# A macaron block on one Trainium2 core: the recurrent cell worked in column halves, with its operands taken straight from PSUM

## The reference

```python
def ffn(x):                                    # x: (2, 4096, 512)
    S  = slot_init * slot_scale                # 64 slots x 512, the same for both batches
    h  = gelu(cat(x, mean(S)) @ w1.T + b1)
    alpha = top-8 softmax of (h @ w2.T + b2) / (|tau| + 0.1)       # (2, 4096, 64)
    gi = einsum('bts,btd->bsd', alpha, x) / (alpha.sum(1) + 1e-8)  # 128 rows x 512
    gx, gh = gi @ gru_wih.T + gru_bih, S @ gru_whh.T + gru_bhh
    r, z = sigmoid(xr + hr), sigmoid(xz + hz)
    n  = tanh(xn + r * hn)
    S_new = (1 - z) * n + z * S
    return alpha @ (S_new @ wv.T + bv) @ wo.T + bo
x = x + 0.5 * ffn(layernorm(x)); x = x + attention(layernorm(x)); x = x + 0.5 * ffn(layernorm(x))
```

## Time and profile before

| | us |
|---|---|
| median of 3 runs | 3148.35 |
| lowest, highest | 3143.83, 3149.79 |
| the profiled execution's own time | 3147.79 |
| its span, first to last instruction | 3146.0 |
| PE busy, DVE busy | 2772.3, 1968.4 |
| ACT busy, POOL busy | 1034.5, 1333.4 |

### The profile page before, as it was taken

One profiled execution on the slowest core, in us unless ns is written; L12 is line 12 of the kernel. 1 busy time (PEld: TensorE's weight loads), 2 busy tenths in 40 slices (PEclk: granted clock), 3 DMA queues, 4 the chain that ended last, 5 costly groups with the idle time before them and its releaser, 6 DMA issues.

```text
span 3146.0 us, 119389 instructions
## 1 busy us (share of the span) xinstructions
PE 2772.3 (88%) x51036; PEld 1964.7 (62%) x51036; DVE 1968.4 (63%) x5236; ACT 1034.5 (33%) x1891; POOL 1333.4 (42%) x1768
## 2 busy tenths in 40 slices
PE   7999788888898999989989988999888999888867
PEld 5786456666666666666666666666666666666553
DVE  6776456566666666666666665666666666666625
ACT  5775223233333332323233322333333332323220
POOL 2221344444444444444445544544454444444410
PEclk9999899999999999999999999999999999999978
DMA  6341122222111222212222222222111222211177
GB/s 220 96 154 48 39 53 58 53 58 57 44 43 53 58 58 57 58 52 56 50 58 58 56 53 58 58 54 55 39 51 54 58 58 58 61 50 48 40 247 282
DMA packets 365979, 224.93 MB, mean 71 GB/s; under 512 B 277584, under 2 KB 294032, under 8 KB 365456
## 3 DMA queue, kind: packets, MB, share of 16 engines
q1 hardware_dynamic: 356240, 200.51, 23.1%
q10 hardware_dynamic: 9216, 16.78, 1.4%
HBM read 125.49 MB, written 74.97 MB: 64 GB/s over the span
## 4 chain that ended last, share of the span: by engine, by line
PE 51%; DVE 31%; issue 11%; POOL 2%; DMA 2%; ACT 1%; SPq 1%; DVEq 0%; POOLq 0%; ACTq 0%
DVE blk L3164 12%; PE psum L887 10%; DVE blk L3162 9%; PE psum L1067 4%; PE psum L983 4%; PE psum L1086 4%; PE psum L1008 4%; PE psum L1043 4%; PE psum L1053 4%; PE psum L963 2%; PE psum L1021 2%; PE psum L1107 2%; PE psum L942 2%; POOL sm L2490 1%; PE psum L791 1%
## 5 line engine op out<-in xcount | busy, mean ns | idle before, releaser
L887 PE MATMUL psum<-w_all,xnT 128*128 128x512 f32 (+2 forms) x2048 | 747.7, 501 | 16.5 <-DVE xc L3061 12.3
L2490 POOL TENSOR_TENSOR sm<-sm,half 128x1 f32<-128x1 f32 (+1 forms) x384 | 537.4, 1399 | 146.1 <-ACT sm L2065 130.1
L887 PEld LDWEIGHTS psum<-w_all,xnT 128*128 128x128 f32 x2048 | 364.4, 191 | 185.9 <-issue 140.5
L3164 DVE TENSOR_TENSOR blk<-blk 128x30 f32<-128x30 f32 (+14 forms) x960 | 452.4, 471 | 33.0
L3162 DVE TENSOR_TENSOR blk<-blk 128x30 f32<-128x30 f32 (+14 forms) x960 | 362.4, 378 | 69.7 <-issue 42.8
L942 PEld LDWEIGHTS psum<-xnT,w_all 128*128 128x128 f32 x2048 | 268.3, 200 | 80.5 <-issue 76.1
L942 PE MATMUL psum<-xnT,w_all 128*128 128x128 f32 x2048 | 292.8, 289 | 7.8 <-issue 7.8
L1067 PE MATMUL psum<-qg,st 32*32 32x64 f32 x8192 | 189.0, 227 | 92.2 <-DVE st L3180 51.7
L1086 PE MATMUL psum<-w_out,gate 128*128 128x512 f32 x512 | 264.4, 636 | 1.2 <-issue 1.0
L1067 PEld LDWEIGHTS psum<-qg,st 32*32 32x32 f32 x8192 | 143.8, 111 | 174.4 <-issue 167.5
L3180 DVE STREAM_TRANSPOSE st<-psum 128x128 f32<-128x128 f32 x256 | 81.0, 316 | 230.3 <-PE psum L1067 227.3
(11 more groups left out here) (276 smaller groups left out, 4694.8 us busy)
## 6 DMA issues: line engine op xcount, KB each, us to landing
blk<-n_scratch SPq DMA_DIRECT2D x64, 512.0 KB, 4.4
xin<-in_L_attn_x_dram SPq DMA_DIRECT2D x96, 256.0 KB, 4.2
xh<-xc SPq DMA_DIRECT2D x64, 256.0 KB, 2.3
n_scratch<-nn SPq DMA_DIRECT2D x64, 256.0 KB, 3.5
e_scratch<-blk SPq DMA_DIRECT2D x32, 512.0 KB, 2.6
E<-e_scratch SPq DMA_DIRECT2D x64, 256.0 KB, 3.9
x_scratch<-xh SPq DMA_DIRECT2D x62, 256.0 KB, 2.6
rxn<-in_L_attn_x_dram SPq DMA_DIRECT2D x32, 256.0 KB, 2.8
```

The lines of the kernel that those rows point to most:

```text
L887: last = mm(dst, xnT[b][:, k * P:(k + 1) * P], w_all[:, k * WK + at:k * WK + at + n], start=(k == 0), stop=(k == KC - 1))
L2490: return g.tensor_tensor(dst, a, half[:, 0:n], ALU.pow)
L3164: ins = tt(Y[:, 0:rows, s_ + 1:CH], Y[:, 0:rows, s_ + 1:CH], o, ALU.add)
```

## The change

The cell works in halves of 256 columns (`HC`) where a step waits for a step. The scaling reads the sums directly from PSUM, in two instructions; the transposes go two blocks at a time into two different banks (`turned`), and ACT copies each half. The z product is made as two products of 256 columns into two banks (`z_at`), and its sums, sigmoids and the last two DVE operations are done by halves. The bias of n is added to r times h_n ahead of the n product's end instead of behind it. `value(k)` are the four blocks of the last product. The last step's slot sums no longer go through ACT and POOL: DVE adds them out of PSUM. The memsets of `slotacc`, `st` and `sums` move from behind the first cell into it. ACT gets two 1x1 activations (`ask`), which place the table loads for Gelu and Exp in the last step of the attention pass.

```diff
+        turned = [Bk[0], C[1]]
+        z_at = [A[1][:, 0:HC], ST[0][:, 0:HC]]
...
                 e.wait_ge(mid_dve, o_dve + 1)
                 e.wait_ge(aT, NT * (m + 1))
-                for k in range(KC):
-                    last = tr(Bk[0][:, k * P:(k + 1) * P], ht[:, k * P:(k + 1) * P], ident[:, :])
-                last.then_inc(mid_pe, 1)
-                e.wait_ge(mid_act, o_act + 1)
+                turn(0)
+                e.wait_ge(mid_dve, o_dve + 2)
+                turn(1)
...
+                gate_product(A[0][:, :], 0, 0, D)
+                gate_product(C[0][:, :], 2, 0, D)
+                gate_product(z_at[0], 1, 0, HC)
+                gate_product(z_at[1], 1, HC, HC)
                 e.wait_ge(mid_dve, o_dve + 7)
+                turn(0)
+                e.wait_ge(mid_act, o_act + 7)
+                value(0)
+                e.wait_ge(mid_dve, o_dve + 8)
+                turn(1)
+                value(1)
+                e.wait_ge(mid_act, o_act + 8)
+                value(2)
+                value(3).then_inc(mid_pe, 1)
...
-            sp.wait_ge(mid_pe, 6 + 4)
+            sp.wait_ge(mid_pe, 9 + 6)
...
+                if n == NT and b == 0:
+                    act(ask[0:1, 0:1], eps[0:1, 0:1], ACT.Gelu).then_inc(asked, 1)
...
-            def slot_sums(m, rows, total):
-                ve.wait_ge(last_sums, m + 1)
-                own(v.tensor_copy(slotacc[:, D:D + 1], total))
-                own(v.tensor_copy(slotacc[:, 0:D], rows))
...
+                for c in (lo, hi):
+                    ts(ht[:, c], rows[:, c], s(0, "rden"), None, ALU.mult).then_inc(mid_dve, 1)
+                if m == 0:
+                    own(v.memset(slotacc[:, 0:D], 0.0))
+                    for b in range(B):
+                        own(v.memset(st[b][:, :], 0.0))
+                    own(v.memset(sums[:, :], 0.0))
...
-            ve.wait_ge(S["sla"], NT)
+            ve.wait_ge(S["sla"], NT - 1)
+            ve.wait_ge(S["slot_ps"], both(NT, 1))
+            own(tt(slotacc[:, 0:D], slotacc[:, 0:D], slot_at[:, :], ALU.add))
```

More of the change, by code:

```diff
@@ L81, in build @@
         eps = sb("eps", 1)
+        ask = sb("ask", 1)
         h_bias = sb("h_bias", 2)
@@ L338, in build, with turn, gate_product, value @@
         NMID = 4
+        HC = D // 2
+        turned = [Bk[0], C[1]]
+        z_at = [A[1][:, 0:HC], ST[0][:, 0:HC]]
         def mid(e, m):
-            o_pe, o_act, o_dve = 6 * m, 5 * m, 7 * m
+            o_pe, o_act, o_dve = 9 * m, 8 * m, 9 * m
             if e is nc.tensor:
                 mm, tr = nc.tensor.matmul, nc.tensor.transpose
+                def turn(h):
+                    for k in range(2):
+                        last = tr(turned[h][:, k * P:(k + 1) * P], ht[:, (2 * h + k) * P:(2 * h + k + 1) * P], ident[:, :])
+                    last.then_inc(mid_pe, 1)
+                def gate_product(dst, j, c, n):
+                    for k in range(KC):
+                        if j == 0 and k % 2 == 0:
+                            e.wait_ge(mid_act, o_act + 1 + k // 2)
+                        last = mm(dst, giT[:, k * P:(k + 1) * P], wihT_at(k, j)[:, c:c + n], start=(k == 0), stop=(k == KC - 1))
+                    last.then_inc(mid_pe, 1)
+                def value(k):
+                    return mm(Bk[1][:, :], hTT[:, k * P:(k + 1) * P], voT_at(k), start=(k == 0), stop=(k == KC - 1))
@@ L358, in mid @@
[L358 to L366, removed]
@@ L373, in mid @@
+                e.wait_ge(mid_dve, o_dve + 3)
                 act(gr[:, :], gr[:, :], ACT.Sigmoid).then_inc(mid_act, 1)
-                e.wait_ge(mid_dve, o_dve + 3)
+                e.wait_ge(mid_dve, o_dve + 4)
                 act(gn[:, :], gn[:, :], ACT.Tanh).then_inc(mid_act, 1)
[L376 to L379, removed]
+                for h in range(2):
+                    e.wait_ge(mid_dve, o_dve + 5 + h)
+                    act(gz[:, h * HC:(h + 1) * HC], gz[:, h * HC:(h + 1) * HC], ACT.Sigmoid).then_inc(mid_act, 1)
@@ L381, in _ @@
+                for h in range(2):
+                    e.wait_ge(mid_pe, o_pe + 7 + h)
+                    act(hTT[:, h * HC:(h + 1) * HC], turned[h][:, 0:HC], ACT.Copy).then_inc(mid_act, 1)
         @block.sync
@@ L2116, in last_exp @@
             def last_exp(n, b):
+                if n == NT and b == 0:
+                    act(ask[0:1, 0:1], eps[0:1, 0:1], ACT.Exp).then_inc(asked, 1)
                 sc.wait_ge(S["top"], both(n + NT, b))
@@ L2609, in slot_add @@
             def slot_add(n):
+                if n == NT:
+                    return
                 pl.wait_ge(S["slc"], n)
@@ L3704, in _ @@
             for b in range(B):
-                own(v.memset(st[b][:, :], 0.0))
                 own(v.memset(D33[b][:, :, 0:1], 0.0))
-            own(v.memset(sums[:, :], 0.0))
             first_dve()
```

56 lines of the change are left out of this document (27 added, 29 removed).

## The result

| | runs | median us | lowest, highest |
|---|---|---|---|
| before | 4 | 3149.07 | 3143.83, 3152.06 |
| after | 4 | 3111.75 | 3108.68, 3117.82 |

The ratio is 0.9886, 95% interval 0.9865 to 0.9907. The forecast was 3139.3, with a range from 3134.0 to 3146.0. Of all executions reported here, four between 5174 and 12049 us were disturbed and are left out. The profiled execution of the changed kernel took 3109.64 us and has a span of 3107.8, against 3146.0 before, 38.2 less.

The account below looks back on a forecast made before the run. One engine works at a time through each cell, so cuts there leave the total: 1.49 + 1.84 + 0.64 + 1.28 + 1.84 = 7.1 us, plus 2.0 for the clock, 9.1 us. Forecast 3139.3, range 3134 to 3146.

Parts of the forecast that it names:

- First cell, entry: First cell, DVE's first copy to the first product pass: scaling from PSUM and half transposes and copy gain 1.49 us.
- First cell, tail: First cell, end of the products to the last product: half operations gain 2.06 us, less 0.22 for two transposes: 1.84.
- Behind the first cell: Between first cell and the attention pass's first sum: moving DVE's 1.87 us of memsets away gains 0.64 us.
- Second cell, entry: Wait into the second cell and its steps before the products: DVE starts 0.25 us earlier, 1.28 us gained in all.
- the store that is late next: Ahead of the second cell: SP's store of the tile before, 4.9 us to land, holds ACT's `aT_out` copy; 0.28 more without it.
- Second cell, tail: Second cell, end of the products to the last product: gain 2.30 us, less 0.46 for two slow transposes: 1.84.
- The clock: PE's products in both cells: shorter gaps give back 0 to about 7 us lost to half clock; 2 us taken.
- The rival that the clock stays up in both cells: Both cells: shortened gaps no longer cost a half-clock stretch, 7.1 + 6 or 7 us, about 3135; chance 0.12.
- The rest: ACT's early table loads for Gelu and Exp: 0 us for both, bounds -0.3 and 0.
- The attention pass: The 32 steps between the cells: no gain counted; a shift of PE's instruction stream should average out.
- a rival for the worse: Attention pass: shifted PE instruction fetch makes the steps slower, at 0.5 us a step 3155; chance 0.08 that it eats the gain.
- a little luck: Attention pass: a favourable shift of PE's stream, as much luck as the other way, left within the forecast's range.

Follow-up runs that it names:

- The tiles' place: Kernel before plus only the unused one-column tile `ask` behind `eps`, moving every tile behind it by 32 bytes: 12.9 ± 2.8 us faster, ratio 0.996.
- The 16 instructions: Kernel before plus 16 PE semaphore signals of no effect in the first cell's gap behind the z product: 5.7 ± 2.1 us faster, ratio 0.998.
- The trace with a gap of 3.28 us: Changed kernel with the first cell's z product left whole instead of in halves: 24.7 ± 4.1 us faster than the kernel before, ratio 0.9922.

## Why the prediction was wrong

**What holds the time together.** The three comparisons of the changed kernel (36.0, 27.6 and 30.4), weighted by their errors, give 32.7 ± 1.9 us. One pair of traces gave 14.9 to the cells and what lies behind them, but parts of the second cell differ from execution to execution, so I take the means over all traces: the first cell gives 7.2 and the second 5.7, together 12.9. The tiles' place gives 12.9 ± 2.8 in the kernel before, 0.8 of it in the last loop. The 16 instructions give 5.7 ± 2.1 there. The sum is 31.5 ± 3.5. The first two parts are clear of noise. The third rests on a difference of 2.7 errors and on other shifts of the stream that gave other times. In the changed kernel the tiles' place is worth 32.7 - 14.4 = 18.3 ± 3.0, which leaves less for the stream; the two splits agree within their errors and no better.

**First cell, entry: right.** 1.91 and 1.34 us became 0.94 and 0.91, gain 1.40; forecast 1.49.

**First cell, tail: right.** 4.35 us became 2.28, less 0.22 for the transposes inside the last product: 1.85; forecast 1.84.

**Behind the first cell: right.** From the last product's end to the first sum, 2.64 us became 1.99 (319.17 to 321.16): 0.65; forecast 0.64. The moved memsets are hidden.

**Second cell, entry: the place was right, the size was not.** The steps in the cell gained 0.38 and 0.54, forecast 0.34 and 0.69. I named the store that is late next, and it was. But I gave it the 4.9 us of the earlier trace rows, and it took 6.94; why is not shown. From PE's last slot product DVE's start comes after 5.93 us, where it was 4.02 (3065.85 in the trace of before, to 3069.87): in this pair 1.9 later and not 0.25 earlier. Over all traces it is neither: from that product to DVE's reciprocal it is 4.4 to 7.3 us in the 12 with the cell of before and 4.4 to 6.7 in the 6 with the changed cell and the shared tile, 5.6 in the mean of each.

**Second cell, tail: right.** 4.81 us became 2.28, less 0.22: 2.31; forecast 1.84, because I reckoned with slow transposes and they ran at full clock. In 4 of the 12 traces with the cell of before they ran at full clock there too, so the mean gain is 2.2.

**The clock: mechanism right, term mis-sized.** The prediction said "I take 2 us, nearer to nothing". In the pair of traces it is 6.7: products 1.57 and 1.20, last products 1.69 and 2.27. In the means over all traces it is 5.9: 1.6 and 0.6, 1.7 and 2.0. The rival that the clock stays up in both cells gave 6 to 7, and it is what happened, but for the second cell's first products, which it had against it. My reason for only 2 us was that "where PE's clock changes relative to the work differs from execution to execution". In the first cell that is wrong. In all 12 traces with the cell of before, its products took 12.0 to 12.3 us and the last product, from first start to last end, 5.40. In the 7 with the cell of after and z in halves these are 10.59 and 3.92 each time. In the second cell it is right for the products: 12.0 to 13.4 us before and 11.7 to 12.9 after. The last product there took 5.4 to 6.0 before and 3.92 after, each time. The trace with a gap of 3.28 us shows the other side of the step. The Trainium skill (TensorE: Matmul & The Clock Gate, the HAM clock gate) says that the clock follows PE's recent activity; the traces agree, and I should have let its rival weigh more.

**The rest: right.** The load for Gelu is hidden before and after, and neither `ask` shows in the chain but for 0.2 us ahead of the last exponentials.

**The attention pass: the step that failed.** The cells gave 12.9 us by the means, and that alone would have put the time at 3135.5, inside the range. The other 19.8 ± 1.9 come from the pass, but for 0.8 in the last loop. The prediction put the pass at no change and had only a rival for the worse on it. It said of PE's stream that "the pattern already falls at other places in each step, so a shift should average out". The runs speak against it. A step has 3131 instructions, 59 more than a multiple of 256, so the edges do wander through the step. The share of stalls at the edges stays the same (103 of 210 and 107 of 198). Yet 16 more brought 6 us, 64 more cost 7 and 6 at two places of the program (the second not clear of noise once the late start is taken off), and 16 beyond the changed kernel's cost 10 to 12. Perhaps a wandering pattern repeats in 32 steps too seldom to even out; no run shows that. And since I thought of it only as a loss, its gain was left to "a little luck".

The larger part, 12.9 ± 2.8 us for the tile's 32 bytes, the prediction did not consider at all. It treated `ask` as two activations and not as a tile that moves 64 others. The diff shows its line, and the load's packets of 128 bytes were there to be looked at.

**Open.** Which accesses lose when the tiles lie 32 bytes beside a multiple of 64. E's load is one, 0.7 us each, but it brought only 3.4 ± 2.5 us. The store from `nn` and the last loop are two more; the three don't add up to 12.9 in the time. Nor is it known which edge of a block costs what in a step; I know the sums, not the places.

## What to carry to other kernels

A new tile, however small, is an edit to every tile behind it. Read the addresses of before and after modulo 64, try an unused tile first when a kernel moves 128-byte packets, and put small tiles last or together.

In a kernel whose PE runs tens of thousands of small instructions, a change in their number ahead of a long loop can move its time by several microseconds either way. Each shift here was only just clear of its noise, so this is a reading and not a law. A gain or loss of 0.2% in such a kernel is no verdict on the edit until the same edit has been timed with the stream shifted.

Where one engine works at a time, measure the gap ahead of a dense stretch, not only its work: here 2.3 us instead of 3.3 kept the clock and was worth more than the operations saved.

## What the runs showed of the hardware that was not expected

The 256 KB load of E in packets of 128 bytes lands after 3.1 to 3.3 us in the 9 traces in which E starts at a multiple of 64 bytes, and after 3.8 to 4.1 in the 11 in which it starts 32 beside one (medians of 64 loads each). Its packets take 12.9 ns in the former and 14.7 to 15.0 in the latter, at 96 and at 160 modulo 256 alike.

A semaphore signal of no effect takes PE's sequencer 0.151 us, where I had reckoned 0.05. At the start, where nothing is queued, they showed; behind 24 product passes, 64 and even 70 of them (9.7 and 10.6 us) left the cell at 24.21 us, since the sequencer runs that far ahead of the array.

Executions of one kernel differ by 5 to 10 us (standard deviation), so the 6 us between lowest and highest of the three that stood ahead of the prediction told little. Differences under 5 us needed a dozen runs and were not always settled by them.
